# Attention scores and row maxima: two maps at once in two 64-row halves of the array, 48-row products, maxima over 1024 columns per instruction

## What is computed

```
q = (xn @ Wq) -> 32 maps of 8 numbers, k = (xn @ Wk) -> 16 of 8, v = (xn @ Wv) -> 8 of 16, rotary on q and k
s = q k^T * 8**-0.5, causal mask, p = softmax(s); o = p v          # each key group (KVH = 8) serves 4 maps of q
attn = o_map1 - lambda * o_map2, rms norm over 16, @ Wo
```

## Time and profile before

| What | Value |
|---|---|
| Runs | 2002.34, 1993.98, 2000.56 us; median 2000.56 |
| Profiled execution, first to last instruction | 2000.2 us |
| Its own time | no other time is listed for it; the span lies 0.4 us below the median of the runs |
| PE busy | 1869.5 us (93%) |
| DVE busy | 1456.6 us (73%) |
| ACT busy | 1050.9 us (53%) |
| POOL busy | 670.8 us (34%) |
| Mean granted TensorE clock | 0.971 of full speed |
| DVE maxima L1768 | 1536 instructions, 763.4 us busy |
| PE maxima L885, scores L900 | 1536 each, 505.2 and 500.8 us |

### The profile page before, as it was taken

One profiled execution on the slowest core, in us unless ns is written; L12 is line 12 of the kernel. 1 busy time (PEld: TensorE's weight loads), 2 busy tenths in 40 slices (PEclk: granted clock), 3 DMA queues, 4 the chain that ended last, 5 costly groups with the idle time before them and its releaser, 6 DMA issues. The chain is left out here.

```text
span 2000.2 us, 42093 instructions
## 1 busy us (share of the span) xinstructions
PE 1869.5 (93%) x11851; PEld 1116.7 (56%) x11851; DVE 1456.6 (73%) x3474; ACT 1050.9 (53%) x2538; POOL 670.8 (34%) x730
## 2 busy tenths in 40 slices
PE   7888999999999999999999999999899999999985
PEld 4543434444343444434444347777688888788874
DVE  7898888988888888888888854444367865433347
ACT  3325567676676666666666644344333323344445
POOL 4542441111111232322223213777703443133324
PEclk9877899999999999999999999999999999999998
DMA  4443342212222121212212102443322211354247
GB/s 129 138 144 103 99 114 71 71 25 71 59 63 80 46 62 40 65 41 59 55 45 62 42 15 85 124 124 111 111 74 88 74 51 54 111 170 141 86 159 150
DMA packets 196455, 170.42 MB, mean 85 GB/s; under 512 B 92120, under 2 KB 176392, under 8 KB 195976
## 3 DMA queue, kind: packets, MB, share of 16 engines
q1 hardware_dynamic: 173064, 115.75, 20.9%
q0 software_dynamic: 20128, 50.35, 8.0%
q10 hardware_dynamic: 3168, 3.15, 0.6%
HBM read 104.16 MB, written 76.90 MB: 91 GB/s over the span
## 5 line engine op out<-in xcount | busy, mean ns | idle before, releaser
L1768 DVE TENSOR_REDUCE mx<-ps 128x1 f32<-128x512 f32 (+3 forms) x1536 | 763.4, 549 | 106.1 <-PE ps L889 85.5
L1358 ACT ACTIVATE fbuf<-ps 128x512 f32<-128x512 f32 (+3 forms) x1024 | 459.4, 507 | 255.6 <-PE ps L900 251.3
L885 PE MATMUL ps<-rbuf 72*128 72x512 bf16 (+3 forms) x1536 | 505.2, 336 | 32.8 <-DVE mx L1768 19.9
L900 PE MATMUL ps<-rbuf 75*128 75x512 bf16 (+3 forms) x1536 | 500.8, 333 | 21.1 <-DMA rbuf<-mrows 18.3
L900 PEld LDWEIGHTS ps<-rbuf 75*128 75x128 bf16 x1536 | 150.3, 98 | 328.0 <-ACT fbuf L1358 138.0
L1358 ACT ACTIVATE gbuf<-ps 128x512 f32<-128x512 f32 (+2 forms) x512 | 211.3, 469 | 102.0 <-PE ps L900 100.9
L732 POOL TENSOR_SCALAR_AFFINE_SELECT gbuf<-gbuf 128x512 f32<-128x512 f32 x96 | 61.4, 640 | 530.3 <-ACT gbuf L1358 530.3
L885 PEld LDWEIGHTS ps<-rbuf 72*128 72x128 bf16 x1536 | 151.9, 99 | 146.3 <-DVE mx L1768 102.9
L915 PE MATMUL ps<-fbuf 128*32 128x512 f32 (+3 forms) x2048 | 228.8, 519 | 2.1 <-issue 0.2
L889 PE MATMUL ps<-maskq,identb 128*128 128x128 bf16 x1024 | 230.1, 225 | 0.0
L739 POOL DMA_INDIRECT y_scr<-wstage,bidx x138 | 138.8, 1006 | 242.2 <-ACT wstage L1402 218.9
(11 more groups left out here) (271 smaller groups left out, 2961.4 us busy)
## 6 DMA issues: line engine op xcount, KB each, us to landing
rbuf<-q_scr SPq DMA_DIRECT2D x192, 96.0 KB
xs_scr<-in_pad SPq DMA_DIRECT2D x8, 1360.0 KB, 6.4
gbuf<-xs_scr SPq DMA_DIRECT2D x69, 136.0 KB, 2.2
gbuf<-xe_scr SPq DMA_DIRECT2D x69, 136.0 KB, 2.1
rbuf<-k_scr SPq DMA_DIRECT2D x192, 48.0 KB
gbuf<-y_scr SPq DMA_DIRECT2D x8, 1024.0 KB, 5.3
q_scr<-gbuf SPq DMA_DIRECT2D x48, 128.0 KB
gbuf<-a_scr SPq DMA_DIRECT2D x12, 512.0 KB, 4.7
```

What stands on the lines that cost most here:

```text
L885: ins = pe.matmul(o, qst[par][0:PROWS, i // 4, m, P * (i % 4):P * (i % 4 + 1)], kst[par][0:PROWS, m % 2, 512 * piece:512 * piece + width], ...
L900: pe.matmul(o, kst[par][0:SROWS, m % 2, P * j:P * (j + 1)], qst[par][0:SROWS, h, m, t0:C], start=True, stop=True).then_inc(b_scores, 1)
L1358: act.activation(prob(s)[:, t0:C], ps[:, s % SRING, t0:C], ACT.Exp, scale=SCALE).then_inc(b_exp, 1)
L1768: dve.tensor_reduce(mx[:, i // 4, piece, n:n + 1], ps[:, SRING + s % SRING, 0:width], AX, ALU.max, negate=True).then_inc(b_maxed, 1)
```

## The change

- The products of parts are 6 instead of 9: `PROWS = 48`, 51 with the maximum's rows. Two maps that use different rows of `k` lie in rows 0 to 50 and rows 64 to 114 of `qst` and `kst`, and their matmuls are issued one behind the other into different banks. `scores` issues pairs (24 to a unit) and increments once for a pair; the ring stays at three banks.
- Maxima: 18 instructions to a unit, each over two banks (1024 columns), filled by 2, 4, 8 or 12 matmuls. The mask of four diagonal tiles is added by 4 matmuls of 512 columns from `identh` and `maskh`. Two slots of two banks replace the ring of three. The turned maxima and outputs, which had a bank of their own, go through the same slots: 22 slots in `ORDER`, one to a score pair, with pauses at pairs 7 and 23. Missing entries of `mx` are preset, and a DVE `tensor_reduce` over four columns makes `mfull` for each half.
- Slot 0 of a unit, which stands behind its first score pair, is now the first maximum tile of the next unit (before: behind the sixth score tile). `OT_A` stands at pair 16 (before: score tile 29 of 48), `SHIFT_A` at pair 12 (before: tile 33).
- `load_q` and `load_k` issue 10 DMAs per half instead of 6: 8 of them read a block of DRAM twice by a broadcast dimension, 2 are plain. `store_shift(u, 1)` moves ahead of `load_v`.
- Around it: `wq` is rearranged by 4 copies for 2, the masks take 6 `affine_select` for 2, the router's counts are copied out of PSUM at once (`take_ranks`), the fold steps of the last unit are respaced.

```diff
-PROWS = PARTS * PARTS * HD
+PROWS = 6 * HD
+ROWS = 64
-MAXJ = [(i, 0, m) for i in range(4) for m in range(MAPS)] + \
-       [(i, p, m) for i in range(4, 8) for p in range(2) for m in range(MAPS)]
+MAXJ = [("diag", 0, 0), ("diag", 0, 2), ("two", 2, 0), ("two", 3, 0), ("four", 0, 1)] + \
+       [("one", i, r) for i in range(4, 8) for r in range(REPS)] + \
+       [("diag", 1, 0), ("diag", 1, 2), ("two", 6, 512), ("two", 7, 512), ("four", 1, 1)]
+ORDER = [0, 1, SHIFT_B, 2, 3, 4, 5, OT_B, 6, 7, 8, SHIFT_A, 9, 10, 11, OT_A, 12, 13, 14, 15, 16, 17]
+STEP_OF = [k + (k >= 7) for k in range(len(ORDER))]
-SHIFT_B_AT, OT_B_AT, OT_A_AT, SHIFT_A_AT = 9, 14, 29, 33
...
+            def load_q(u, par, h, landed):
+                for s in range(2):
+                    own = q_scr[h, :, :, u, s].rearrange("a d r t -> a d (r t)")
+                    to = qst[par][:, h].rearrange("p r t -> p (r t)")
+                    sp.dma_start(to[ROWS * s:ROWS * s + 32],
+                                 own[0:2].rearrange("a d t -> (a d) t").unsqueeze(0).broadcast_to((2, 2 * HD, REPS * C))
+                                 ).then_inc(landed, 16)
+                    sp.dma_start(to[ROWS * s + 32:ROWS * s + PROWS], own[0::2]).then_inc(landed, 16)
+            def load_k(u, par, h, landed):
+                ts = slice(C * h, C * (h + 1))
+                for s in range(2):
+                    own = k_scr[:, :, u, s, ts]
+                    for a in range(2):
+                        sp.dma_start(kst[par][ROWS * s + 16 * a:ROWS * s + 16 * (a + 1), ts],
+                                     own[1 + a].unsqueeze(0).broadcast_to((2, HD, C))).then_inc(landed, 16)
+                    sp.dma_start(kst[par][ROWS * s + 32:ROWS * s + PROWS, ts],
+                                 own[0:2].rearrange("a d t -> (a d) t")).then_inc(landed, 16)
             def load_qk(u, par, reuse=None):
-                for h in range(2):
-                    ...
+                if reuse is not None:
+                    sp.wait_ge(b_scores, PAIRS * reuse - (PAIRS - 2 * LATE))
+                load_q(u, par, 0, b_qk_in[par])
+                load_k(u, par, 0, b_qk_in[par])
+                if reuse is not None:
+                    sp.wait_ge(b_scores, PAIRS * reuse)
+                load_q(u, par, 1, b_q_in[par])
+                load_k(u, par, 1, b_k_in[par])
...
             def unit(u, par, first, last):              # SP
                 if not last:
                     load_qk(u + 1, 1 - par, None if first else u)
+                store_shift(u, par, 1)
+                if not last:
                     load_v(u + 1, 1 - par)
-                store_shift(u, par, 1)
...
+            def max_matmuls(u, par, w, bank):           # PE
+                kind, i, at = MAXJ[w]
+                if w == 0:
+                    pe.wait_ge(b_qk_in[par], 160 * (u // 2 + 1))
+                if w == MAXA:
+                    pe.wait_ge(b_q_in[par], 64 * (u // 2 + 1))
...
+                if kind == "diag":
+                    for c in range(2):
+                        for s in range(2):
+                            rows = slice(ROWS * s, ROWS * (s + 1))
+                            pe.matmul(ps[:, bank + s, :]..., identh[rows, c], maskh[rows, c]..., start=(c == 0), stop=False)
+                    for r in range(REPS):
+                        for d in range(2):
+                            for s in range(2):
+                                last = piece(s, 2 * P * r + P * d, q, r, P * q, P, False, r == d == 1)
+                elif kind == "one":
+                    for s in range(2):
+                        last = piece(s, 0, i, at, 0, C)
...
+            def unit(u, par, first, last):              # PE
+                for t in range(PAIRS):
+                    scores(u, par, t, first)
+                    if not last and t in STEP_OF:
+                        slot(u, par, STEP_OF.index(t), first)
...
+                    if t % REPS == REPS - 1:
+                        values(...)
...
+            def reduce_max(u, w, bank):                 # DVE
+                dve.wait_ge(b_maxs, MAXS * u + w + 1)
+                both = ps[:, bank:bank + 2, :]
...
+                dve.tensor_reduce(to, of, AX, ALU.max, negate=True).then_inc(b_maxed, 1)
+                if w in (MAXA - 1, MAXS - 1):
+                    dve.wait_ge(b_maxed, MAXS * u + w + 1)
+                    dve.tensor_reduce(mfull[:, h], mx[:, h].rearrange("p c n -> p n c"), AX, ALU.min
+                                      ).then_inc(b_mfull, 1)
```

More of the change, by code:

```diff
@@ L900, in scores @@
[L900 to L906, removed]
+                for s in range(2):
+                    rows = slice(ROWS * s, ROWS * s + SROWS)
+                    last = pe.matmul(ps[:, (2 * t + s) % SRING, t0:C], kst[par][rows, P * j:P * (j + 1)],
+                                     qst[par][rows, h, r, t0:C], start=True, stop=True)
@@ L912, in values @@
                 else:
[L913 removed]
+                    pe.wait_ge(b_exp, JOBS * u + MAPS * (g + 1))
                 t0 = max(0, P * j - C * h)
[L915 to L923, removed]
@@ new lines, in slot @@
+            def slot(u, par, k, first):
+                what, bank = ORDER[k], MX + 2 * ((k + 1) % 2)
+                slot_free(u, k)
+                if what == SHIFT_B:
+                    turn_shift(u, 1, bank)
+                elif what == SHIFT_A:
+                    turn_shift(u + 1, 0, bank)
+                elif what == OT_B:
+                    if first:
+                        rank(bank)
+                    else:
+                        turn_ot(u - 1, 1, bank)
+                elif what == OT_A:
+                    turn_ot(u, 0, bank)
+                else:
+                    max_matmuls(u + 1, 1 - par, what, bank)
@@ L967, in unit @@
+                    if t % REPS == REPS - 1:
+                        g = t // REPS
+                        if g >= LAG:
+                            values(u, par, g - LAG, first)
+                        elif not first:
+                            values(u - 1, 1 - par, len(GROUPS) + g - LAG, False)
+                    if last and t in FOLD_AT:
+                        e = FOLD_AT.index(t)
                         if e < NE:
@@ L1868, in _, with unit @@
-            for s in range(LEAD):
-                reduce_max(0, s)
-                if s == MAXA + 4:
-                    shift_rows(0, 0, 0, True)
-            unit(0, 0, True, False)
+            def unit(u, par, first):
+                for k, what in enumerate(ORDER):
+                    bank = MX + 2 * ((k + 1) % 2)
+                    if what == SHIFT_B:
+                        shift_rows(u, 1, par, first, bank)
+                    elif what == SHIFT_A:
+                        shift_rows(u + 1, 0, 1 - par, False, bank)
+                    elif what == OT_B:
+                        if first:
+                            take_ranks(bank)
+                        else:
+                            combine_maps(u - 1, 1, False, bank)
+                    elif what == OT_A:
+                        combine_maps(u, 0, first, bank)
+                    else:
+                        reduce_max(u + 1, what, bank)
+                    if first and k == SELECT_AT:
+                        chosen(0)
+                    if first and k in ROUTE_AT:
+                        route(0, ROUTE_AT.index(k))
@@ new lines, in last_unit @@
+            def last_unit(u, par):
+                for t in range(PAIRS):
+                    what = LAST_ORDER.get(t)
+                    if what == SHIFT_B:
+                        shift_rows(u, 1, par, False, TAIL)
+                    elif what == OT_B:
+                        combine_maps(u - 1, 1, False, TAIL)
+                    elif what == OT_A:
+                        combine_maps(u, 0, False, TAIL)
+                    if t in FOLD_AT:
+                        fold(FOLD_AT.index(t))
```

343 lines of the change are left out of this document (174 added, 169 removed).

## The result

The changed kernel takes 2147.19 us (median of four runs, 2136.66 to 2154.58) against 2001.45 of the kernel before on the same chip: ratio 1.0734, 95% interval 1.0697 to 1.0771. It is slower by 7.3%. The forecast was 2080 with a range of 1910 to 2200. Times are medians of all runs and ratios are of runs in the faster of two states alone, which matters only for experiment 2, where three of twelve runs were in the slower one.

What follows compares the result with a forecast made beforehand. PE set the old pace, DVE close behind; in the new kernel late loads through SP's queue would. From 2000.2 us, +54 for thirty units, +21 for pads and about +5 for the first unit gave 2080 us, range 1910 to 2200.

Steps and rivals of the forecast that it cites:

- loads that close the loop: SP's late q and k loads set the unit: 33.4 us with low clock, against 31.6; +54 us over 30 units; chance 0.55.
- path after `OT_A`: SP's queue from DVE's output to the next unit's first load, through output store and shift stores: 3.0 us.
- ten loads: SP's first-half q and k loads: 7.6 us of issue and about 1.4 to land, 9.0 us.
- chain and clock: DVE from slot 0's fill to the output of OT_A, 20.4 us, plus 1.0 for the slow clock after the stall.
- The pads: Pad stores ahead of the loads in seven units make them land later: 7 x 3.0 = +21 us.
- The first unit: Late loads with no predecessor to hide them, needed earlier and 3 us longer: about +5 us.
- the work in the projections: POOL's added copies and selects and DVE's presets lie under SP's stores: no cost.
- the chain: DVE walking all slots of a unit in order: 28.4 us if nothing else waits.
- The second half's shift rows: SP's shift stores behind ten loads land some 10 us into a unit, where pair 8 needs them: priced at nothing.
- Short loads: Rival: SP's loads take 5.4 us and DVE's 28.4 us is the unit; 1904 us, up to 1930; chance 0.27.
- One half after another: Rival: PE's row halves do not run side by side, about 35 us a unit; 2130 us; chance 0.10.
- Clock stays low: Rival: PE at half clock for three quarters of a unit, about 39 us; 2220 to 2400 us; chance 0.08.

Runs made afterwards that it cites:

- experiment 2: Changed kernel, same loads reordered on SP: first half's q and k issued two units ahead, before the output of OT_A is stored; 2001.93 us, ratio 0.9982.
- Experiment 1: Changed kernel without the q and k loads of units 2 to 31, which reread those of units 0 and 1; 1945.01 us, ratio 0.9709.
- experiment 3: Changed kernel, first half's q and k loads two units ahead, second half's shift rows stored between its q and k loads; 1935.61 us, ratio 0.9667.
- experiment 7: Changed kernel with both maps of a pair in the same rows, so its matmuls cannot run side by side; 2868.77 us, ratio 1.4320.

## Why the prediction was right, and where it was small

*Mechanism.* The forecast, loads that close the loop, is what the trace shows, and experiments 1 and 3 confirm it: with the same engines' work and no late load the kernel is faster than before. The direction was right; the size was not, +135 us against a forecast of +80.

*The loop.* In the unit at 929 us: path after `OT_A` 3.0 predicted, 3.36 measured; ten loads 9.0, measured 9.27 (7.22 issue, 2.05 to the use); chain and clock 20.4 + 1.0, measured 21.8 together. No term is far off, but all three are short, and a unit is 34.4 instead of 33.4. This term was +54 and measured 30 x 2.83 = +85. That the loads came out so near is partly luck: two of the eight said to read a doubled dimension are plain, and cost as much.

*The pads.* 7 x 3.0 = +21 counted seven units, where eight have a pad store, and was set against a kernel before with 31.6 us everywhere. Measured: eight units 37.9 us over the ordinary ones, three long units without a pad store another 9.6, less 16.4 by which the units of the kernel before themselves exceed 31.6: +31. The three long units have the clock at 0.78 to 0.86 on average by the trace, where most ordinary ones have 0.90 to 0.95 (870 to 885 us above). Most units with a pad store have a lower clock too, 0.76 to 0.91, so the +31 is loads and clock together.

*The first unit.* I priced it at +5 and the work in the projections at nothing; together they are +17.6. The step that failed is "POOL's added copies and selects ... lie in the projections, under SP's stores", which looked at the wrong thing: in SP's queue the projections' later stores begin at 74.73 us instead of 68.90. Of these 5.8 us, 1.7 arise ahead of the first loads (61.49 against 59.80) and the rest in twenty loads instead of twelve. The first unit then waits 6.9 us for its successor's loads, with the clock at 0.57 in 150 to 200 us (0.77 before). How the 17.6 us divide beyond that is not shown; experiments 1 and 3, which keep the first unit's loads, keep it (first output at 198.7 and 198.3).

*Sum.* 85 + 31 + 17.6 + 1.0 for the tail against 54 + 21 + 5: 135 against 80.

*DVE and PE.* The maxima take 1.22 us where 1.18 was worked out from 1.03 ns a column, and the shortest units without late loads take 28.1 to 28.2 where the chain was 28.4. With 1.22 the same sum gives 29.1, so a part of that match is luck. PE's 22.8 us were too low: in experiment 3 it is in work for 821 of 950 us, 25.3 in an average unit of 29.3. It sets the pace no longer, as forecast.

*The second half's shift rows* were priced at nothing, "if they are late, a microsecond a unit is lost". In the changed kernel the loop hides them; in experiment 2, with the loop gone, that is the wait that came next. Without it the 30 units are 71 us shorter, more than the 32 us of the wait itself; the clock went from 0.91 to 0.96 with it, which may be the rest.

*The rivals.* Short loads (1904 to 1930): its condition is not met, but its price nearly is; with the loads in time the kernel takes 1936. One half after another (2130): near the measured time, and still wrong; 0.39 us for a pair and the pairs of experiment 7 rule it out. Clock stays low (2220 and more): not as a state of the whole stretch, which has 0.88; in the long units it is part of the loss.

## What to carry to other kernels

When work is made narrower, look at the order in which one queue issues stores and loads: here the same instructions and transfers give 1.073 or 0.967 of the old time, by the order of loads and stores in SP's queue. Place a load behind the last reader of its buffer, not behind the outputs that happen to be stored earlier in the code. After one late transfer is mended, ask which row of that queue is late next: the second one held back some 65 of the 212 us that lie between 2147 and 1936.

## What the runs showed of the hardware

An engine in work all the time may still have the lower clock: the kernel before with 48 rows in its score and maximum matmuls had 0.50 over 950 us with PE in work for 950, where 72 and 75 rows had 0.99; pairs of 48 rows, issued into two halves of the array, ran at 1.00 between their waits. The Trainium skill, "TensorE: Matmul & The Clock Gate", What's actually happening, describes the clock by how busy the engine has been; the 48-row run does not agree, and the measurement decides. Which property of those matmuls it was beyond the number of rows was not tried.

In experiment 2 a wait of 1.4 us was followed by nearly 14 us at the lower level (824 to 838 us: 0.50 to 0.56). In the changed kernel a wait of 5.0 us was followed by about 3 us of it at 942, and one of 5.3 us by some 13 at 870. Experiment 1 has no wait for a load, and 0.94 all the same; there the units grow from 28.2 to 29.7 and 30.7 us as their mean clock goes from 1.00 to 0.94 and 0.89. Neither the length of a wait nor its absence tells what the clock costs; what made it fall or last in each case is open.
